# The high f16 halves of q and k move from GpSimd to VectorE, and the tables that weave an attention and FFN kernel are set anew

## The reference, cut to what matters

```python
x = x + _layernorm(_L0_attn_ref(_layernorm(x), Wq, Wk, Wv, Wo, W_down_kv, W_up_k, W_up_v))
x = x + _layernorm(_L0_ffn_ref(_layernorm(x), ffn_weight))

# attention: 16 heads of 16
q, k, v = x @ Wq, x @ Wk, x @ Wv
latent_kv = (k + v) @ W_down_kv              # 64 wide
k_rec, v_rec = latent_kv @ W_up_k, latent_kv @ W_up_v
scores = einsum('bhqd,bhkd->bhqk', qh, kh) * scale          # clip, then
scores = scores * exp(-1e-4 * |i - j|)                      # decay, clip
out = softmax(scores) @ vh ; return out @ Wo

# ffn
xh = x @ H                                   # 256 x 256 Hadamard
xq = clip(round(xh / s), -8, 7) * s          # s = max|xh| / 7 per token
return xq @ ternary(weight).T
```

## Time and profile before

| | us |
|---|---|
| median of 3 runs | 1568.07 (1565.24 to 1568.29) |
| the profiled execution | 1565.73 |
| its span, first to last instruction | 1563.8 |
| TensorE busy | 1389.1 (89%) |
| ScalarE busy | 1162.5 (74%) |
| VectorE busy | 1107.5 (71%) |
| GpSimd busy | 911.5 (58%) |

### The profile page before, as it was taken

One profiled execution on the slowest core, in us unless ns is written; L12 is line 12 of the kernel. 1 busy time (PEld: TensorE's weight loads), 2 busy tenths in 40 slices (PEclk: granted clock), 3 DMA queues, 4 the chain that ended last, 5 costly groups with the idle time before them and its releaser, 6 DMA issues.

```text
span 1563.8 us, 35962 instructions
## 1 busy us (share of the span) xinstructions
PE 1389.1 (89%) x12330; PEld 587.4 (38%) x12330; DVE 1107.5 (71%) x2604; ACT 1162.5 (74%) x1252; POOL 911.5 (58%) x1188
## 2 busy tenths in 40 slices
PE   5789998999999999999999999999999999999842
PEld 3223333433433343333333433433343343334321
DVE  5547777777777777777777777777777777776643
ACT  0677877878787787878778787877778787778822
POOL 4335665655666665557666655766665566656233
PEclk9899999999999999999999999999999999999975
DMA  5355455455455545645554555555455555545320
GB/s 167 126 156 156 149 170 156 147 177 179 155 162 169 161 150 168 187 149 157 169 171 151 161 185 153 155 168 179 147 157 184 164 156 165 179 144 160 95 66 28
DMA packets 174540, 241.44 MB, mean 154 GB/s; under 512 B 28320, under 2 KB 145184, under 8 KB 174496
## 3 DMA queue, kind: packets, MB, share of 16 engines
q1 hardware_dynamic: 140160, 206.78, 43.2%
q10 hardware_dynamic: 34336, 34.08, 6.7%
HBM read 154.80 MB, written 69.21 MB: 143 GB/s over the span
## 4 chain that ended last, share of the span: by engine, by line
PE 36%; POOL 25%; DVE 14%; issue 8%; DMA 8%; SPq 6%; ACT 1%; POOLq 0%; DVEq 0%
PE heads_ps L641 13%; PE scores_ps L628 8%; SPq L421 6%; DVE ln_stats L1025 5%; PE misc_ps L530 5%; DMA den_spread<-den_scratch 4%; POOL out_sb L976 4%; POOL ln_rstd L928 4%; POOL xn L946 4%; POOL q_hl L967 3%; POOL k_hl L967 3%; DVE x L1100 3%; DMA den_scratch<-den_inv 3%; PE misc_ps L571 2%; POOL k_hl L965 2%
## 5 line engine op out<-in xcount | busy, mean ns | idle before, releaser
L838 ACT ACTIVATE probs<-scores_ps 128x1024 f32<-128x1024 f32 x768 | 777.1, 1025 | 312.1 <-PE scores_ps L628 308.0
L641 PE MATMUL heads_ps<-probs,v_sb 128*32 128x512 f32 x4096 | 533.1, 604 | 36.9 <-ACT probs L845 33.8
L1162 DVE TENSOR_TENSOR diagonal<-scores_ps,comp 128x1024 f32<-128x1024 f32 x256 | 310.6, 1213 | 175.8 <-PE scores_ps L628 175.3
L628 PE MATMUL scores_ps<-q_rep,k_rep 64*128 64x128 f16 (+2 forms) x5120 | 363.1, 252 | 47.1 <-ACT probs L838 27.5
L628 PEld LDWEIGHTS scores_ps<-q_rep,k_rep 64*128 64x128 f16 x5120 | 157.1, 94 | 505.9 <-issue 279.3
L845 ACT ACTIVATE probs<-diagonal 128x2048 f32<-128x2048 f32 x128 | 243.9, 1906 | 0.0
L972 POOL TENSOR_TENSOR heads_c<-heads_c,den_spread 128x1024 f32<-128x1024 f32 x32 | 75.7, 2366 | 231.6 <-DMA den_spread<-den_scratch 231.6
L1079 DVE SCALAR_TENSOR_TENSOR weighted<-misc_ps,edges 128x384 f32<-128x384 f32 x256 | 130.3, 551 | 66.7 <-PE misc_ps L541 66.3
L921 POOL TENSOR_TENSOR ln_neg_mean<-zero,ln_moments 128x4 f32<-128x4 f32 x128 | 37.9, 296 | 208.6 <-DVE ln_moments L1033 208.6
L641 PEld LDWEIGHTS heads_ps<-probs,v_sb 128*32 128x32 f32 x4096 | 87.8, 108 | 174.7 <-issue 145.7
L965 POOL TENSOR_TENSOR q_hl<-weighted,zero 128x768 f16<-128x768 f32 x64 | 94.3, 1473 | 92.7 <-DVE weighted L1079 92.7
(11 more groups left out here) (110 smaller groups left out, 1555.2 us busy)
## 6 DMA issues: line engine op xcount, KB each, us to landing
q_rep<-q_scratch SPq DMA_DIRECT2D x128, 384.0 KB, 3.8
k_rep<-k_scratch SPq DMA_DIRECT2D x256, 192.0 KB, 4.4
q_scratch<-q_hl SPq DMA_DIRECT2D x64, 384.0 KB, 2.3
k_scratch<-k_hl SPq DMA_DIRECT2D x64, 384.0 KB, 3.0
x_in<-in_L_attn_x_dram ACTq DMA_DIRECT2D x32, 512.0 KB, 3.6
heads_c<-heads SPq DMA_DIRECT2D x256, 64.0 KB, 2.3
x_res<-in_L_attn_x_dram ACTq DMA_DIRECT2D x32, 512.0 KB, 4.9
den_spread<-den_scratch SPq DMA_DIRECT2D x256, 64.0 KB, 2.4
```

Source lines behind the costliest of these rows:

```text
L628: ins = mm(scores_ps[:, place + par, at:at + n * P], k_rep[rows, pair, kv_, k_cols], q_rep[rows, pair, qv_, q_cols], start=True, stop=True)
L641: ins = mm(heads_ps[W32 * g:W32 * (g + 1), :], v_sb[:, b.slot, kt, at:at + W32], probs[:, quad % 2, g, kt, :], start=(kt == 0), stop=(kt = ...
L838: nc.scalar.activation(flat[:, :, at:at + S], scores_ps[:, place:place + 2, :], ACT.Exp, scale=EXP_SCALE).then_inc(off_probs, 1)
L1162: v.tensor_tensor(diagonal[:, quad % 2, 2 * two:2 * two + 2, :], scores_ps[:, place:place + 2, :], comp[:].rearrange("p t n -> p (t n)").u ...
```

## The change

1. `weigh` on VectorE gets one more instruction behind its two: a `tensor_copy` of the 768 weighted columns from f32 in SBUF into the high f16 half, after a wait for its own weighing and for the spread of the batch before. `split` on GpSimd keeps only the subtraction.
2. Separate semaphores for the stores of q and of k; `spread` issues the two DMAs of q first and waits for k's store only then.
3. The five tables are set anew. On TensorE more score units stand in pairs (20 groups of units in an iteration, 23 before), z is cut into two pieces, the second half of y is one piece, and qintT stands after unit 26 instead of 29.
4. In the opening, VectorE makes the ternary weights behind the first q and k instead of ahead of them, and takes v after the path is decided; `up_weights` is cut in two, and the last part of `path_choice` is cut into three functions in another order.

```diff
-    0: [("z", 0, 0), ("z", 1, 0)], 2: [("pv_end", 3, 0), ("pv_end", 3, 1), ("pv_end", 3, 2)], 4: [("xT", 0, 0)], 5: [("xT", 1, 0)],
+    0: [("z", 0, 0)], 1: [("z", 1, 0), ("pv_end", 3, 0)], 3: [("xT", 0, 0), ("pv_end", 3, 1)], 5: [("xT", 1, 0), ("pv_end", 3, 2)],
...
-POOL_STEPS = ["rstd4", "x1_apply", ("q", 0), ("k", 0), "heads_normalize", ("k", 1), "add_out", "x_apply", ("q", 1), "rstd2"]
+POOL_STEPS = ["rstd4", "x1_apply", ("q", 0), ("k", 0), ("k", 1), "heads_normalize", "x_apply", "add_out", ("q", 1), "rstd2"]
...
             def spread(b, c):
...
-                sp.wait_ge(qk_stored[c], 16 * STORES * (b.number + 1))
+                sp.wait_ge(q_stored[c], 16 * (b.number + 1))
...
                 for again in range(2):
                     sp.dma_start(q_rep[again:P:2, mine].rearrange("p a v n -> p a (v n)"), q_rows).then_inc(rep_spread[c], 16)
+                sp.wait_ge(k_stored[c], 16 * (b.number + 1))
+                for again in range(2):
                     for hl in range(2):
                         sp.dma_start(k_rep[2 * again + hl:P:4, mine].rearrange("p a v n -> p a (v n)"), k_rows[hl]).then_inc(rep_spread[c], 16)
...
             def split(b, name, c):
                 at = SPLITS.index((name, c))
                 hl = q_hl if name == "q" else k_hl
-                pool.wait_ge(taken[name], part_count(name, b, c))
-                if not (isinstance(b.number, int) and b.number == 0):
-                    pool.wait_ge(rep_spread[c], 16 * SPREADS * b.number)
                 src = weighted[:, at % 2]
-                nc.gpsimd.tensor_tensor(hl[:, c, 0], src, zero[:].to_broadcast([P, SPAN]), ALU.add).then_inc(high_done, 1)
                 pool.wait_ge(high_done, count(len(SPLITS), b, at + 1))
                 nc.gpsimd.tensor_tensor(hl[:, c, 1], src, hl[:, c, 0], ALU.subtract).then_inc(split_done, 1)
...
                 ins.then_inc(taken[name], 1)
+                dve.wait_ge(taken[name], part_count(name, b, part))
+                if not (isinstance(b.number, int) and b.number == 0):
+                    dve.wait_ge(rep_spread[part], 16 * SPREADS * b.number)
+                hl = q_hl if name == "q" else k_hl
+                v.tensor_copy(hl[:, part, 0], weighted[:, at % 2]).then_inc(high_done, 1)
...
                     xT_take(b, part)
-                ternary_weights()
                 dve.wait_ge(second_loaded, 16 * SECOND)
                 weigh(b, "q", 0)
                 lat_take(b, 0)
                 weigh(b, "k", 0)
+                ternary_weights()
                 weigh(b, "k", 1)
+                take_ternary()
+                diagonal_tables()
+                weigh(b, "q", 1)
+                x_stats(b.other(1))
+                x_moments(b.other(1))
+                path_choice()
                 for part in range(2):
                     v_take(b, part)
-                x_stats(b.other(1))
-                x_moments(b.other(1))
-                weigh(b, "q", 1)
-                path_choice()
```

More of the change, by code:

```diff
@@ L79 @@
+    27: [("qintT", 0)],
 }
 VECTOR_STEPS = {
-    0: [("z", 0)], 2: [("z", 1), ("x1_make",), ("z_stats",)], 3: [("x1_stats",), ("z_moments",)], 4: [("x1_moments",)],
-    5: [("xT", 0), ("xT", 1)], 7: [("lat", 0)], 9: [("heads_end", 3)], 11: [("q_split", 0)],
-    14: [("x1_low", 0), ("x1_low", 1), ("k_split", 0), ("k_split", 1), ("den_invert",)], 16: [("v", 0)], 17: [("heads", 0)],
-    19: [("act_scales",)], 20: [("v", 1)], 26: [("x_stats",), ("x_moments",), ("heads", 1), ("y", 0), ("q_split", 1), ("quantize",)],
@@ L85 @@
-    31: [("y", 1), ("y_stats",), ("y_moments",), ("heads", 2)],
-}
-POOL_STEPS = ["rstd4", "x1_apply", ("q", 0), ("k", 0), "heads_normalize", ("k", 1), "add_out", "x_apply", ("q", 1), "rstd2"]
-SYNC_STEPS = [("own", "spread", 1), ("a", "gather_den"), ("a", "pack_den"), ("a", "compact", 1), ("a", "return_den"),
-              ("pre", "store_q", 0), ("pre", "store_k", 0), ("a", "spread_den"), ("pre", "spread", 0), ("own", "compact", 0),
-              ("pre", "store_q", 1), ("pre", "store_k", 1), ("c", "store_out")]
+    0: [("z", 0)], 1: [("z", 1), ("x1_make",)], 2: [("xT", 0)], 3: [("z_stats",)],
@@ L92 @@
+SYNC_STEPS = [("own", "spread", 1), ("a", "gather_den"), ("a", "pack_den"), ("pre", "store_q", 0), ("a", "compact", 1),
+              ("a", "return_den"), ("a", "spread_den"), ("pre", "store_k", 1), ("pre", "store_k", 0), ("pre", "spread", 0),
+              ("c", "store_out"), ("pre", "store_q", 1), ("own", "compact", 0)]
 ORDER_ALL = [step for h in sorted(TENSOR_STEPS) for step in TENSOR_STEPS[h] if step[0] in PARTS]
@@ L691, in latent_weights, with up_weights @@
                 ins.then_inc(setup_pe, 1)
[L693 to L698 removed]
+            def up_weights(w, up):
+                for ci in range(DC):
+                    ins = mm(scores_ps[:, 2 + w, ci * D:(ci + 1) * D], w_latT[:, ci * P:(ci + 1) * P], up[0:LAT, :], start=True, stop=True)
                 ins.then_inc(setup_pe, 1)
@@ L991, in opening_batch @@
                 x_apply(b)
-                for name, c in SPLITS[:3]:
+                for name, c in SPLITS:
                     split(b, name, c)
                 x_apply(b.other(1))
-                split(b, *SPLITS[3])
             opening_batch(Batch(0, 0, 2))
```

65 lines of the change are left out of this document (33 added, 32 removed), and 10 rows, old and new, of the table TENSOR_STEPS.

## The result

The changed kernel takes 1475.74 us (median of 4, 1474.84 to 1477.54) against 1568.18 us for the kernel before on the same chip: ratio 0.941, 95% interval 0.9386 to 0.9434. The gain is 92 us, not 61.

A forecast was written before the change was run, and what follows sets the result against it. TensorE, close to full, bounds the middle: 42.1 us of work plus 1.5 of waits saves 1.85 us per iteration, 52 us; early iterations and 31 add 3, opening 4, tail 2: 61 us, so 1507 us, range 1478 to 1552.

The forecast's parts named there:

- Sum 2.92 us. The other 42.5 us are TensorE's own work.: TensorE's middle iteration of 45.46 us: six bracketed waits total 2.92 us, the rest is its own work.
- the six waits: TensorE's waits before units 5, 6, 17, v, z and the last weighted sums of the batch before; 2.92 us in all.
- Turns: TensorE in the middle: fewer switches between score units and other work save 0.3 us, 0.4 with y and z.
- New waits: TensorE in the middle: 1.0 us before unit 6, 0.2 at x1's transposes, 0.3 at k; 1.5 us in all.
- Iterations 0 to 2: Early iterations: 1 and 2 have the middle's waits with fewer stages, gaining 1 us each.
- The opening: Before the first unit: weights and tables computed in VectorE's gaps, v after the decision; 4 us less, bounds 0 and 6.
- with the clock as it was: Opening: the walk to a cast at 39 us, 4 us less, assumed an unchanged clock.
- The copies: VectorE's four high-half copies per batch: 0.55 us each when free, 3.3 us in all, bounds 2.2 and 11.7.
- rival 1: Between third and fourth diagonal: copies and GpSimd operations block each other, each iteration 2.15 us longer, 1619 us; 10%.
- Rivals 2 and 3: 2: VectorE later at unit 6, 1532 us, 22%. 3: ScalarE keeps TensorE waiting as before, 1548 us, 10%.
- rival 4: Middle: unit 6 is not late, no wait appears, 42.1 us an iteration, 1465 us; 8%.

The follow-up runs named there:

- the light one: Kernel before with layer norm statistics over 64 of 256 values and exponentials over half their columns: 1529.3 us (one run), period 43.82 us.
- the old opening: Changed kernel with the opening order of before; tables, VectorE's copies and split semaphores stay new: 1480.02 us, ratio 0.942.
- the copy only: Kernel before with only VectorE's copy of the high halves added, GpSimd keeping the subtraction; tables and opening as before: 1575.12 us, ratio 1.003.
- three pairs broken: Changed kernel with three pairs of score units broken by moving pv 1,1, y 0 and the second row of y 1: 1510.97 us, ratio 0.963.
- the high halves on GpSimd: Changed kernel with the copy undone, high halves back on GpSimd; tables and opening stay new: 1477.37 us, ratio 0.941.
- one join: Kernel before with pv 1,1 and 1,2 both behind unit 20, so units 21 and 22 become a pair: 1582.56 us, ratio 1.009.
- one wait removed: Kernel before with qintT one unit earlier on TensorE and ScalarE, removing the wait before z: 1571.42 us, ratio 1.002.
- x1 first: Changed kernel with x1 ahead of z on VectorE, GpSimd and ScalarE: 1464.05 us; then with z_apply at 14, 15, 18, 18: 1452.24 us.

## Why the prediction was wrong

The mechanism was right: the order of the tables makes the gain, on TensorE, in the middle; the clock stayed at 1.00; the wait for the second diagonal before units 6 and 7 is the largest. The sizes were off, and those of the middle nearly all in one direction.

**The step that failed** is "Sum 2.92 us. The other 42.5 us are TensorE's own work." A bracket holds less than the wait costs. From start to start the six waits cost 0.38, 0.35, 0.43, 0.36, 0.66 and 1.19 against 0.31, 0.28, 0.34, 0.29, 0.58 and 1.12, 3.37 in all. As all six went, the 0.45 went with them. The forecast names the reason and uses it for the work alone: starts lie closer together than listed durations, and a bracket counts from the listed end. The rows of the full kernel and of the light one both show 42.0 to 42.1 of work and 3.3 to 3.4 of waits in its place.

**Turns.** Three turns fewer at 0.1 each were to give 0.3, and 0.4 with y and z; by the rows it was 0.6 (42.0 to 41.4). Joining shortens what stands on the other side of the units too, and the sum had counted this for y alone. q1 directly ahead of y takes 3.65 with it (707.28 to 710.93) against 1.92 and 1.93 apart, 0.2 less. x1's turn in one piece takes 1.03 (734.58 to 735.61) against twice 0.59, 0.15 less:

```profile
733.08 0.66 PE L571 MATMUL misc_ps<-ident,y_sb 128*128 128x128 f32 x4
733.67 0.39 PE L628 MATMUL scores_ps<-q_rep,k_rep 64*128 64x256 f16 x4
```

Around k some 0.1 of this is lost again (a unit ahead of k took 0.23 and 0.24 before).

**New waits.** 1.5 forecast. Before units 6 and 7 it is 0.77 instead of 1.0; at x1's turn 0.2, as forecast; before k 0.1 instead of 0.3; and two that were not in it, 0.2 at the pair behind qintT and 0.1 elsewhere. In all 1.4: right in sum.

So the period fell by 0.6 + 3.4 - 1.4 = 2.6 us instead of 0.4 + 2.9 - 1.5 = 1.85. Over 28 iterations that is 22 of the 27 us between the forecast and the spans. **Iterations 0 to 2** gave 7.8 us, not 2, and 31 with the tail 5.2, not 3. Nothing was run on these, but the traces show part of it. From the first unit to the first q1 row it is 29.0 us before and 27.5 after; in it the granted clock is 0.50 from 48 to 52 us and 0.70 to 56 us before, 0.79 and then 1.00 after. The next two distances between q1 rows are 42.1 and 43.8 against 38.1 and 41.8, with brackets of 6.0 and 2.6 in them against 4.4 and 1.3. The forecast had taken the waits of the middle for these. Behind them the distances of before go on to 45.0, 46.0 and 46.8, the last two with 0.87 and 1.41 for the diagonal before unit 6; why that one is so late there stays open.

**The opening** was to give 4 and gave 1.2 (first unit 43.23, forecast near 40). The runs do not split this into parts that hold. Starting from before, the copies make the first unit 2.6 later (44.47 to 47.06) and the new order then makes it 3.7 earlier (46.91 with the old opening, 43.23). The other way round, the new order without the copies changes nothing (44.64) and the copies then give 1.4. Each is one execution, and the clock lies over them: 1.8 of the 2.6 is TensorE's clock, since q1 took 3.78 us with the copy only and 1.98 before. In the changed kernel both q rows are slow, and between 28 and 36 us the granted clock is 0.58 where it was 0.84:

```profile
18.12 3.75 PE L533 MATMUL misc_ps<-xT,wq 128*128 128x512 f32 x4 [0.88 <-DVE xT L1041]
...
31.74 3.78 PE L533 MATMUL misc_ps<-xT,wq 128*128 128x512 f32 x4
```

The forecast took the clock as it was, and it differs from run to run in this stretch: with three pairs broken, the same opening, q0 was at full speed (1.96) and the first unit came at 41.48. So what failed here is "with the clock as it was"; what the order alone is worth stays open.

**The copies** at 0.56 to 0.58 median and 0.85 at most are at the low end of 0.55 to 1.1, 2.3 us for the four of a batch instead of 3.3. They were cheap as forecast, but rival 1's premise barely occurs in the loop: the quantizing operation, 1.17 median before, is now 0.68, since GpSimd's addition of the output no longer stands beside it. Either half of the change does that (0.686 with the copy only, 0.683 with the high halves on GpSimd). In the opening the blocking is plain. A VectorE operation on 128x2 elements, 0.17 in the trace of before, ends only when GpSimd's low half does:

```profile
27.07 1.11 DVE L1180 TENSOR_SCALAR xscale<-xscale 128x2 f32<-128x2 f32 x1
```

```profile
26.52 1.64 POOL L964 TENSOR_TENSOR k_hl<-weighted,k_hl 128x768 f16<-128x768 f32 x1 [1.19 <-DVE k_hl L1082]
```

That is the rule of the Trainium skill, "SBUF — State Buffer", section "SBUF: two separate sides", which the prediction gives, and the trace agrees once more: the VectorE operation ends at 28.18 and GpSimd's at 28.16.

**The rivals.** Rival 1 (slower) did not occur: copies that meet a whole low part were not seen. Rivals 2 and 3 looked for later engines; only rival 4 looked the other way, with no wait and 42.1 an iteration (1465). It had 8%, and the range leaves most of it out. It was half right: a wait remained, and the work was less than 42.1. The range was closed at the side where the sum itself was unsure: 0.07 for each of six waits was in the earlier trace rows to be read.

## What to carry to other kernels

Cost a wait by the distance between starts and not by its bracket, and take own work as what is left of the period after that; six waits hid 0.45 us of 45. A turn between kinds of matmuls costs on both sides, so count the join of the long work as well as that of the short. Where several engines hold each other in a ring, one edit only moves the wait (one join made the kernel 0.9% slower, one wait removed gave nothing); move the lists of all engines together, and look after each step for the engine that is late next, as the last two steps with x1 first did, for another 1.6% below the changed kernel. An effect of a few us in the opening can't be read from one trace when the clock there differs from execution to execution.
